# Four tables of the steady pairs: one value pass, the norms' power, three statistics passes and the flip change places

## The reference

```python
xn = _gn(x)                                    # 32 groups of 6 channels, mean and variance over the group
xt = xn.reshape(b, c, n).transpose(0, 2, 1)    # b=16, c=192, n=2304
q, k, v = split(xt @ w_qkv, 3)                 # 8 heads of d=24
q = q / max(sqrt(sum(q * q, axis=tokens)), EPS); k = k / max(sqrt(sum(k * k, axis=tokens)), EPS)
k = k * temperature
attn = softmax(einsum('bhpn,bhnq->bhpq', k, q))      # 24 x 24 per head
out = einsum('bhnp,bhpq->bhnq', v, attn)             # (b, h, n, d)
out = heads_joined(out) @ w_out + b_out
y = x + out.transpose(0, 2, 1).reshape(b, c, H, W)
```

## Time and profile before

| what | value |
|---|---|
| median of 3 runs | 354.87 us (354.72 to 355.15) |
| profiled execution, its own time | 353.76 us |
| its span, first to last instruction | 352.0 us |
| TensorE busy | 311.4 us, 88% |
| VectorE busy | 285.1 us, 81% |
| ScalarE busy | 243.9 us, 69% |
| GpSimd busy | 145.9 us, 41% |
| mean granted clock of TensorE | 0.989 |

### The profile page before, as it was taken

How to read it: one execution, slowest core, us unless ns; L and a number is a source line. 1 busy time by engine, 2 the same in 40 slices (tenths; PEclk the granted TensorE clock), 3 DMA queues, 4 the chain that set the end, 5 groups by cost and what they waited for, 6 DMA issues and landing times.

```text
span 352.0 us, 9368 instructions
## 1 busy us (share of the span) xinstructions
PE 311.4 (88%) x3692; PEld 221.2 (63%) x3692; DVE 285.1 (81%) x705; ACT 243.9 (69%) x447; POOL 145.9 (41%) x129
## 2 busy tenths in 40 slices
PE   0148858999999999999999999999999999999895
PEld 0036636765678666866687567866687567756552
DVE  5899895896889698987899698978899685278874
ACT  1088589758986699759986799759976898740300
POOL 0069679305860178215750387016840586002000
PEclk9999987999999999999999999999999999999999
DMA  7999920005995289815993499627981574016876
GB/s 234 358 313 252 239 72 3 3 2 171 317 313 145 91 251 336 267 47 175 312 331 83 135 290 294 217 102 196 345 286 44 160 233 135 3 47 169 282 225 221
DMA packets 30828, 67.75 MB, mean 192 GB/s; under 512 B 5504, under 2 KB 12096, under 8 KB 30784
## 3 DMA queue, kind: packets, MB, share of 16 engines
q1 hardware_dynamic: 30544, 66.56, 61.0%
q10 hardware_dynamic: 240, 0.59, 0.7%
HBM read 29.38 MB, written 28.31 MB: 164 GB/s over the span
## 4 chain that ended last, share of the span: by engine, by line
issue 35%; POOL 19%; PE 17%; DVE 15%; ACT 8%; SPq 2%; DMA 2%; ACTq 0%; POOLq 0%; DVEq 0%
POOL l_sb L502 14%; PE u_ps L1014 6%; PE g_ps L1014 5%; DVE bnst L798 4%; ACT h_sb L574 3%; PE s_ps L1014 3%; POOL r L519 2%; ACT xn L565 2%; DMA wo<-in_L_conv_w_out_dram 2%; POOL grs L508 2%; DVE s_ps L854 2%; ACT tok L612 1%; DVE lg L852 1%; DVE x_sb L937 1%; PE u_ps L1065 1%
## 5 line engine op out<-in xcount | busy, mean ns | idle before, releaser
L502 POOL TENSOR_TENSOR l_sb<-xn,h_sb 128x768 f16<-128x768 f32 x63 | 102.9, 1652 | 48.8 <-ACT h_sb L574 48.7
L937 DVE SCALAR_TENSOR_TENSOR x_sb<-u_ps,bias,x_sb 128x384 f32<-128x384 f32 x144 | 84.0, 612 | 16.7 <-PE u_ps L1014 16.0
L1014 PE MATMUL g_ps<-tok 128*128 128x64 f16 (+1 forms) x864 | 86.2, 240 | 6.3 <-ACT tok L612 5.8
L1014 PEld LDWEIGHTS g_ps<-tok 128*128 128x128 f16 x864 | 57.1, 99 | 30.1 <-ACT tok L612 9.6
L612 ACT COPY tok<-u_ps 128x384 f32<-128x384 f32 x144 | 64.6, 481 | 15.5 <-PE u_ps L1068 14.5
L1014 PE MATMUL u_ps<-h_sb,ml 128*128 128x384 f16 (+1 forms) x336 | 72.7, 326 | 0.0
L798 DVE BATCH_NORM_STATS2 bnst<-x_sb 128x6 f32<-128x384 f32 x144 | 70.2, 543 | 2.8 <-DMA x_sb<-in_x_dram 2.8
L565 ACT ACTIVATE xn<-x_sb,rb 128x768 f32<-128x768 f32 x60 | 59.5, 1023 | 16.3 <-POOL rb L514 14.0
L574 ACT ACTIVATE h_sb<-x_sb,rb 128x768 f16<-128x768 f32 x63 | 64.1, 1032 | 0.4 <-POOL rb L514 0.4
L1065 PE MATMUL u_ps<-id,h_sb 128*128 128x128 f16 x288 | 49.1, 224 | 7.0 <-DVE l_sb L778 6.2
L1066 PE MATMUL u_ps<-id,l_sb 128*128 128x128 f16 x288 | 49.2, 224 | 0.0
(11 more groups left out here) (149 smaller groups left out, 525.2 us busy)
## 6 DMA issues: line engine op xcount, KB each, us to landing
x_sb<-in_x_dram SPq DMA_DIRECT2D x48, 384.0 KB, 5.6
out_dram<-x_sb SPq DMA_DIRECT2D x48, 384.0 KB, 3.1
out_dram<-x_sb SPq DMA_DIRECT2D x48, 192.0 KB, 3.1
x_sb<-in_x_dram SPq DMA_DIRECT2D x45, 192.0 KB, 4.9
hl<-h_sb SPq DMA_DIRECT2D x48, 96.0 KB, 3.3
hl<-l_sb SPq DMA_DIRECT2D x48, 96.0 KB, 3.4
x_sb<-in_x_dram ACTq DMA_DIRECT2D x3, 192.0 KB, 4.4
w<-in_L_conv_w_qkv_dram SPq DMA_DIRECT2D x1, 288.0 KB, 7.3
```

The lines of the kernel that those rows point to most:

```text
L502: nc.gpsimd.tensor_tensor(l_sb[:, par, t, cols], xn[:, c % XN_RING, :], h_sb[:, par, t, cols], ALU.subtract).then_inc(l_ok, 1)
L937: V.scalar_tensor_tensor(out=xs, in0=block_ps(n), scalar=bias[:, t:t + 1], in1=xs, op0=ALU.add, op1=ALU.add).then_inc(out_ok, 1)
L1014: return nc.tensor.matmul(dst, lhs, rhs, start=start, stop=stop, skip_group_check=True)
```

## The change

Five entries move, in the tables of the steady steps alone.

- `PE_A`: the flip stands behind slot 0 instead of slot 1 (steps 1 to 6).
- `ACT_A`, `ACT_B`: pass x8 leaves the end of phase B and stands in phase A of the next step, behind the copy of slot 3. Around it h6 comes one slot earlier (1), exp one slot earlier (5) and h8 one slot later (7); h7 stays at 4.
- `POOL_B`: the norms' power and `rk` come ahead of subtraction 5 instead of behind it.
- `VEC_B`: the first three of the four statistics passes of pair p+3 come behind results 14, 15 and 16; behind result 17 stand spread and the fourth. Before, one stood ahead of spread and three behind it.

```diff
-PE_A = {1: ["flip"], 8: ["v"], 11: ["m"]}
+PE_A = {0: ["flip"], 8: ["v"], 11: ["m"]}
...
-ACT_A = {2: ["h6"], 4: ["h7"], 6: ["exp", "h8"], 11: ["v"], 14: ["m"]}
-ACT_B = ["x0", "x1", "x2", "h0", "t2", "h1", "t0", "t1", "h2", "x3", "x4", "p", "h3", "h4", "x5", "h5", "x6", "x7", "x8"]
-POOL_B = ["power", 0, 1, 2, 3, 4, 5, "norms", 6, 7, 8]
+ACT_A = {1: ["h6"], 3: ["x8"], 4: ["h7"], 5: ["exp"], 7: ["h8"], 11: ["v"], 14: ["m"]}
+ACT_B = ["x0", "x1", "x2", "h0", "t2", "h1", "t0", "t1", "h2", "x3", "x4", "p", "h3", "h4", "x5", "h5", "x6", "x7"]
+POOL_B = ["power", 0, 1, 2, 3, 4, "norms", 5, 6, 7, 8]
...
-VEC_B = {0: ["gram"], 1: ["var"], 3: ["z"], 5: ["t2"], 7: ["t0", "t1"], 10: ["lo"], 13: ["norms"], 17: ["bn", "spread", "bn", "bn", "bn"]}
+VEC_B = {0: ["gram"], 1: ["var"], 3: ["z"], 5: ["t2"], 7: ["t0", "t1"], 10: ["lo"], 13: ["norms"],
+         14: ["bn"], 15: ["bn"], 16: ["bn"], 17: ["spread", "bn"]}
```

## The result

The changed kernel took 350.0 us (349.63 to 350.32, 4 runs) against 355.01 us of the kernel before (354.72 to 355.41, 4 runs). The ratio is 0.9861, its 95% interval 0.9837 to 0.9885: 1.4% faster, 4.9 us. The forecast was 350.2 us. In two later comparisons with the kernel before the changed kernel had ratios of 0.9898 (0.9876 to 0.9921) and 0.9905 (0.9874 to 0.9935), medians of 351.0 us both times. All three are clear of no change; they amount to 4.9, 3.6 and 3.4 us.

The account below looks back on a forecast made before the run. TensorE was taken to set the pace, with 0.8 us per step of standstill in phase A to win. 5 x 0.82 + 0.57 = 4.67 us; 354.87 - 4.67 = 350.2 us, range 348.9 to 352.6.

Parts of the forecast that it names:

- The copy of slot 0: Start of phase A: without x8 ahead, ScalarE's copy follows the transposes at once and slot 0 starts 0.75 us earlier.
- The stops at slot 7 and v: TensorE in phase A: two stops of 0.24 us each, at slot 7 and at v, disappear in steps 1 to 5.
- The new stop at slot 5: TensorE in phase A: slot 5 waits 0.42 us for its copy, now queued behind x8 and h7 on ScalarE.
- Slot 0 to v in 7.75: TensorE in phase A: 7.75 us from slot 0 to v; gain 0.82 us in steps 1 to 5, 0.57 in step 6.
- The power and x8 need each other: End of phase B: early power delays subtraction 5 from 134.7 to near 136.6, hidden because x8 now starts at 137.3.
- The four changed entries have one answer: Whole change: the entries together give 0.82 us per step in steps 1 to 5, with no work added or removed.
- Let phase B keep its 20.3: Phase B: stays at 20.3 us, so the 0.82 us won in phase A is kept in full.
- ScalarE as the bound: First slots of phase A: x8 costs its whole 0.93 us instead of 0.42; 353.3 us, chance 0.11.
- The flip did not stop TensorE: Rival denied here: behind slot 0, blocked VectorE and GpSimd passes make the flip wait 0.73 us; 351.8 us, chance 0.05.
- The third rival: End of phase B: a late load of chunk (2,0) holds up result 17, the flip and slot 1; 359.8 us, chance 0.05.

Follow-up runs that it names:

- experiment 2: The kernel before with only the new tables of the flip and the statistics passes (`PE_A`, `VEC_B`); 351.83 us, ratio 0.9914.
- Experiment 6: The changed kernel with ScalarE's h7 behind the copy of slot 5 instead of 4 and h8 behind slot 8 instead of 7; 349.07 us, ratio 0.9845.
- experiment 4: The kernel before with only the new `POOL_B`, the power ahead of subtraction 5; 368.22 us, ratio 1.038.
- experiment 5: The changed kernel with the old `VEC_B`, so the statistics passes put back; 349.96 us, ratio 0.9871.
- experiment 11: The changed kernel with h7 behind the copy of slot 5, h8 behind slot 8, and VectorE's table as before the change; 350.11 us, ratio 0.9865.
- experiment 9: The changed kernel with the last 12 of 18 statistics passes of pairs 3 to 7 reading chunk (0,0), waiting for no load; 349.96 us, ratio 0.9873.
- experiment 10: The kernel of experiment 9 with the ScalarE table of Experiment 6; 348.21 us, ratio 0.9827.
- Experiment 3: The changed kernel with the old `POOL_B`, subtraction 5 ahead of the norms' power; 352.19 us, ratio 0.9936.
- experiment 8: The changed kernel measured again with nothing altered, against the kernel before; 351.0 us, ratio 0.9898.

## Why the prediction was right

**The time.** 350.0 us against the forecast of 350.2 is partly luck. The forecast gain was 4.67 us. Phases A gave 4.61, and the timed runs of the first comparison 4.9, but the profiled execution kept 3.6, and the two later comparisons show 3.6 and 3.4 us. What is missing is in the phases B, below.

**The copy of slot 0 (+0.75).** Right. The copy is 0.04 behind its transposes, and slot 0 starts 1.07 us into the phase instead of 1.80 (0.73 earlier) in all six steps.

**The stops at slot 7 and v (+0.48).** Right, and shown apart: experiment 2 has exactly these and not the first. They belong to the softmax, not to x8. How much of it the flip's new place brings and how much that of the statistics passes is not shown.

**The new stop at slot 5 (-0.42).** Right: 0.41. Experiment 6 moves it and leaves 0.17, where 0.16 was worked out.

**Slot 0 to v in 7.75.** Right to the hundredth, which is luck in the last digit. It gave 0.82 us a step in steps 1 to 5 and 0.57 in step 6; the phases say 0.81 to 0.83, and 0.53.

**The power and x8 need each other.** Right, and it is the strongest of the findings: the power moved alone costs 13.5 us, x8 alone brings 0.9, and with both in place the power is worth 0.34 a step. The size of the first was put at 8.6 us ahead of experiment 4, which is 5 us short, for the two reasons given there.

**"The four changed entries have one answer."** Too coarse. The statistics passes' new place adds nothing measurable to this kernel (experiment 5). It counts where TensorE is earlier (experiment 11). Where the power is late it should count too: in experiment 2 spread ends at 136.83, and three passes of 0.46 behind it would put `lg` at 138.2, where it was before. That is worked out and was not run.

**"Let phase B keep its 20.3."** This is the step that failed, in one step of the profile. I checked the loads of chunks (0,0) and (2,0), whose passes had moved, and not those of the chunks whose passes had not moved but come 1.1 to 1.2 us earlier. About 0.9 of this is the shorter phase A, the rest the three passes that VectorE no longer has ahead of the softmax (experiment 5 takes it back). In the kernel before, chunk (1,2) had 0.22 or 0.23 us to spare in two steps of five, and chunk (2,1) 0.04 in one. The price is 0.67 us in the first profile, 0.2 in the second, and 0.5 in phase A with 0.84 in phase B in the third. Experiments 9 and 10 show that the loads are the cause.

Whether they also explain the medians of 350.0 and of 351.0 for the same kernel is not shown. Without the waits the runs lie within 0.8 us (experiment 10) and 1.3 us (experiment 9), with them within 0.7, 1.9 and 3.9 us. But the first set has the lowest median although its profile lost 0.67 us, and the slow executions of the other sets, up to 353.35 us, were not profiled.

**The rivals.** ScalarE as the bound did not come: slots 4, 6 and 8 start 0.78 behind the slots before them, without a stop. The flip did not stop TensorE: the passes that ran beside the power took 0.55 each and the power 1.67 (1.65 before), so they did not hold each other up. Experiment 3 makes the flip late by 0.73, the stop that this rival's working had, and phase A then grows by 0.33, where the working gave 0.31. The third rival had the right kind of mechanism, a load that lands behind the pass that wants it, at the wrong place: the passes between the last results never waited, those behind slots 5, 9 and 11 did. It was nearer than the row said: the load of chunk (2,0), which had 1.8 us to spare in that row, landed only 0.08 ahead of its pass in step 3 of experiment 8's profile.

The best kernel of this study that computes the reference is that of experiment 6, 349.07 us. Its interval overlaps the changed kernel's; its phases A are shorter by 0.24 us in each step. The next thing to change would be SyncE's order of stores and loads at the end of phase B and in the first slots of phase A, which was not tried. The stores that the load of chunk (1,2) waits for were issued 5.0 and 5.8 us into phase A of step 3, when SyncE had worked through the copies, stores and loads ahead of them in its order.

## What to carry to other kernels

In this kernel a long pass on the engine that feeds TensorE, just ahead of the first thing that it feeds, cost 0.73 us a step. Freeing it was worth little until the next producer in the chain was early too: move such entries together, and test them apart. When a phase gets shorter, go through the producers whose time does not shrink with it, the loads above all, and take for each its smallest margin over the steps, not that of the one step you read. One trace is not enough for it: the pass that waited 0.74 us had had 0.94 to spare in the same step before, and those that had had 0.22 did not wait.

## What the runs showed of the hardware that had not been expected

A stop of 2.5 us lowered TensorE's granted clock in two steps of experiment 4 (0.54 over 3.3 us in step 2 and 0.56 in step 5, 1.37 and 1.35 us lost) and not in the four others, which had the same stop and kept 1.00. In the kernels before and after, whose stops in phase A are up to 0.64 us, it is 1.00 in every phase of steps 1 to 6.

The same load, at the same place of each step, lands at different times: that of chunk (1,2) 13.90 to 15.25 us into phase A in one execution of the kernel before, and 13.60 to 15.60 in one of the changed kernel. Part of it comes from the stores that it waits for: they landed 9.13 to 11.31 into the phase before, and 9.45 to 10.88 after.
